# Layer 1: where the tap and slab transfers are issued, and how far TensorE's sums run behind the scan

## What is computed

```python
x = conv_general_dilated(x, conv_w, padding=((2, 2), (2, 2)), feature_group_count=C)
x = silu(x + conv_b[None, :, None, None])
xs = x.reshape(B, C, L)
x_dbl = einsum('kd,bdl->bkl', x_proj_w, xs)
dts, Bs, Cs = x_dbl[:, :R], x_dbl[:, R:R + N], x_dbl[:, R + N:]
delta = softplus(einsum('dr,brl->bdl', dt_w, dts) + dt_b[None, :, None])
log_dA = maximum(delta[:, :, None, :] * A[None, :, :, None], LOG_EPS)
P = exp(cumsum(log_dA, axis=-1))
dB_u = delta[:, :, None, :] * Bs[:, None, :, :] * xs[:, :, None, :]
hs = P * cumsum(dB_u / maximum(P, EPS), axis=-1)
y = einsum('bdnl,bnl->bdl', hs, Cs) + xs * Ds[None, :, None]
```

## Time and profile before

| what | us |
|---|---|
| median of 3 runs | 4020.88 (4011.57 to 4022.5) |
| the profiled execution, own time | 4020.36 |
| its span | 4018.6 |
| of it layer 0 and the start of layer 1 | about 1956 |
| scans of groups 0 to 6, each | 252.9 to 262.3 |
| scans of group 7, behind the loop | 246.9 |

### The profile page before, as it was taken

One profiled execution on the slowest core, in us unless ns is written; L12 is line 12 of the kernel. 1 busy time (PEld: TensorE's weight loads), 2 busy tenths in 40 slices (PEclk: granted clock), 3 DMA queues, 4 the chain that ended last, 5 costly groups with the idle time before them and its releaser, 6 DMA issues. The chain is left out here.

```text
span 4018.6 us, 72697 instructions
## 1 busy us (share of the span) xinstructions
PE 3650.8 (91%) x22358; PEld 2646.6 (66%) x22358; DVE 3106.0 (77%) x4416; ACT 2571.1 (64%) x4292; POOL 2575.8 (64%) x2672
## 2 busy tenths in 40 slices
PE   6999999999999999997899998998989989899776
PEld 6888787979787887877565564664646646466322
DVE  3675758475756667570499998999989989989999
ACT  1463728172735546274688787787778878777754
POOL 0352717162634536270488888888979889888988
PEclk9999999999999999998799898998989989989877
DMA  7546473747465554428565564655546646465222
GB/s 225 170 138 204 104 250 95 251 102 234 109 200 149 164 181 125 149 76 181 130 177 143 162 170 124 172 152 147 164 127 181 169 125 173 129 168 158 86 75 60
DMA packets 383746, 612.84 MB, mean 153 GB/s; under 512 B 199967, under 2 KB 324152, under 8 KB 383048
## 3 DMA queue, kind: packets, MB, share of 16 engines
q1 hardware_dynamic: 383336, 607.74, 53.5%
HBM read 527.35 MB, written 80.28 MB: 151 GB/s over the span
## 5 line engine op out<-in xcount | busy, mean ns | idle before, releaser
L321 POOL TENSOR_TENSOR h_low<-act_h,h_high 128x448 fp32r<-128x448 f32 x448 | 598.0, 1354 | 724.1 <-ACT h_high L520 723.9
L515 ACT ACTIVATE act_h<-ps_up,b 128x448 f32<-128x448 f32 x672 | 408.7, 635 | 728.5 <-PE ps_up L633 728.2
L1348 PE MATMUL ps_y<-h,ident 128*128 128x448 f32 x1344 | 727.1, 629 | 144.3 <-POOL h L1036 113.1
L1036 POOL TENSOR_TENSOR h<-h,c_rows 128x448 f32<-128x448 f32 x672 | 763.7, 1136 | 51.2 <-DVE h L1126 5.7
L1023 POOL TENSOR_TENSOR u<-dxs,b_rows 128x448 f32<-128x448 f32 x672 | 764.5, 1138 | 27.9 <-DVE ps_q L1115 16.8
L1099 DVE TENSOR_TENSOR_SCAN ps_q<-d_a,q_last,ps_q 128x448 f32<-128x448 f32 x576 | 659.5, 1145 | 0.0
L1126 DVE TENSOR_TENSOR_SCAN h<-d_a,h_last,ps_q 128x448 f32<-128x448 f32 x576 | 645.3, 1120 | 0.0
L1300 PEld LDWEIGHTS ps_front<-win,taps 120*112 120x112 f32 x4608 | 540.5, 188 | 149.2 <-issue 147.2
L606 PE MATMUL ps_stage<-win,taps 124*112 124x112 f32 x6144 | 608.3, 261 | 2.7 <-DVE w_low L368 2.7
L606 PEld LDWEIGHTS ps_stage<-win,taps 124*112 124x112 f32 x6144 | 608.1, 178 | 3.2 <-DVE w_low L368 2.8
L1205 ACT ACTIVATE d_a<-delta,log_eps,a_neg 128x448 f32<-128x448 f32 x672 | 503.3, 750 | 114.0 <-DVE h L1126 58.5
(11 more groups left out here) (81 smaller groups left out, 6212.6 us busy)
## 6 DMA issues: line engine op xcount, KB each, us to landing
taps<-in_t_dram SPq DMA_DIRECT2D x192, 896.0 KB, 5.0
taps<-in_t_dram SPq DMA_DIRECT2D x192, 672.0 KB, 4.7
b_rows<-bc_dram SPq DMA_DIRECT2D x224, 224.0 KB, 3.0
c_rows<-bc_dram SPq DMA_DIRECT2D x224, 224.0 KB, 3.1
xres<-in_x_dram SPq DMA_DIRECT2D x224, 168.0 KB, 2.5
x_dram<-x1o SPq DMA_DIRECT2D x224, 168.0 KB, 2.0
x1pad<-x_dram SPq DMA_DIRECT2D x96, 392.0 KB, 6.0
out_dram<-y SPq DMA_DIRECT2D x168, 224.0 KB, 2.6
```

Of the source, the lines that this page charges most:

```text
L321: nc.gpsimd.tensor_tensor(h_low[u % 2][:, t, :], act_h[u % 2][:, t, :], h_high[u % 2][:, t, :], ALU.subtract).then_inc(h_low_ready[t], 1)
L515: nc.scalar.activation(act_h[u % 2][:, t, :], ps_up[t][:, 0:BT], ACT.Gelu, bias=b1[:, t:t + 1]).then_inc(gelu_done, 1)
L1036: nc.gpsimd.tensor_tensor(h[s % H_SLOTS][:, :], h[s % H_SLOTS][:, :], c_rows[n][:, :], ALU.mult).then_inc(hc_done, 1)
L1348: nc.tensor.matmul(total, ident[:, :], h[s % H_SLOTS][:, :], start=False, stop=(n == N - 1)).then_inc(y_added, 1)
```

## The change

Three things change, in layer 1 alone. (1) A slab or tap load is no longer put into SyncE's list five steps ahead in any case, but at `begin_at`: five steps ahead, or the step after the slot's last user is scheduled to be done, whichever is later; the list is sorted by that. (2) In a step, these loads stand at the end, behind the row store, the row loads and the store of y. (3) Y_LAG is 3: TensorE sums, ScalarE's copies of y and the stores of y move one step later. The skip matmul keeps its step (s % 4 = 2), now in a function of its own, behind the sum of that step. The last two stores of a group stand at its end.

```diff
--- before.py
+++ after.py
@@ -80,7 +80,7 @@
 U_SLOTS = 3
 U_AHEAD = U_SLOTS
 H_SLOTS = 6
-Y_LAG = 2
+Y_LAG = 3
 Z_SLOTS = 2
 DA_SLOTS = 7
 DA_LEAD = 5
@@ -952,17 +952,21 @@
                 for load, k, _ in loads[:SLABS]:
                     load(f, False, k)
 
+            def begin_at(load, k, unit):
+
+                last_use = {load_slab: turn_unit, load_taps: conv_unit}[load]
+                slots, pieces = {load_slab: (SLABS, 1), load_taps: (SLOTS2, HALVES)}[load]
+                free = unit_step[last_use[k - slots]] + pieces + 1 if k >= slots else 0
+                return max(unit_step[unit] - AHEAD, free)
+
             def group(g, ahead, first=False):
 
-                todo = loads[SLABS:] if ahead else []
+                todo = sorted(loads[SLABS:], key=lambda load: begin_at(*load)) if ahead else []
                 for s in range(S):
                     b, j = s // STEPS, s % STEPS
                     f, fb = next_band(g, b)
                     if ahead == 2 and s == S - 2 * STEPS:
                         first_slabs(g + 2)
-                    while todo and unit_step[todo[0][2]] <= s + AHEAD:
-                        load, k, _ = todo.pop(0)
-                        load(g + 1, False, k)
                     if ahead or b + 1 < BANDS:
                         if j == STORE_XD_AT:
                             store_xd(f, fb)
@@ -974,7 +978,11 @@
                         load_c(g, b, LOAD_C_NOW[j])
                     if s >= N + Y_LAG + 1 and (s - N - Y_LAG - 1) % N == 0:
                         store(g, (s - N - Y_LAG - 1) // N)
-                store(g, RUNS - 1)
+                    while todo and begin_at(*todo[0]) <= s:
+                        load, k, _ = todo.pop(0)
+                        load(g + 1, False, k)
+                for r in range(RUNS - 2, RUNS):
+                    store(g, r)
 
             assert last > 1
             first_slabs(1)
@@ -1335,15 +1343,17 @@
                 nc.tensor.matmul(z[:, 0:BT], dtw[:, t, :], xd[:, :],
                                  start=True, stop=True).then_inc(z_done, 1)
 
+            def skip_y(g, r):
+
+                b, t = r // TILES, r % TILES
+                pe.wait_ge(y_kept, g * RUNS + max(r - Y_SLOTS + 1, 0) + 1)
+                nc.tensor.matmul(ps_y[r % Y_SLOTS][:, 0:BT], skip[:, t, :], xs[:, t, b * BT:(b + 1) * BT],
+                                 start=True, stop=False)
+
             def add_y(g, s):
 
-                b, t, n = s // STEPS, s % STEPS // N, s % N
-                r = b * TILES + t
-                total = ps_y[r % Y_SLOTS][:, 0:BT]
-                if n == 0:
-                    pe.wait_ge(y_kept, g * RUNS + max(r - Y_SLOTS + 1, 0) + 1)
-                    nc.tensor.matmul(total, skip[:, t, :], xs[:, t, b * BT:(b + 1) * BT],
-                                     start=True, stop=False)
+                n = s % N
+                total = ps_y[s // N % Y_SLOTS][:, 0:BT]
                 pe.wait_ge(hc_done, g * S + s + 1)
                 nc.tensor.matmul(total, ident[:, :], h[s % H_SLOTS][:, :],
                                  start=False, stop=(n == N - 1)).then_inc(y_added, 1)
@@ -1359,6 +1369,8 @@
                             front_waits(g + 1, i)
                     if s >= Y_LAG:
                         add_y(g, s - Y_LAG)
+                    if s % N == Y_LAG - 1:
+                        skip_y(g, s // N)
                     if burst:
                         for i in burst:
                             back(g if s == 0 else g + 1, i)
```

## The result

The changed kernel takes 4042.2 us, the median of 5 runs (4039.39 to 4052.35), beside 4022.5 us (4011.57 to 4038.22) for the kernel before, run in between. The ratio is 1.0056, with a 95% interval of 1.0032 to 1.0081: slower by about half a per cent, where 4015 us was forecast and the range ended at 4031. The ratios are not quotients of the two medians; each leaves out executions more than 1.5% above the quickest of their kernel, which drops four of twelve for the loads with the logarithm in front, one of twelve for the last kernel with an extra matmul, and none elsewhere. The profiled execution took 4039.4 us (span 4037.6), against 4020.4 us before.

The account below looks back on a forecast made before the run. VectorE's scans plus stops, ended by ScalarE's logarithm, were taken as the bound. Gains of 3.7 + 1.0 us at steps 8 to 20 and 1.0 at step 72, 5.7 off 4020.4, gave 4014.7, said as 4015; range 3995 to 4031.

Parts of the forecast that it names:

- The reading of what bounds the kernel: VectorE bounds each group, plus its stops; at step 7 the last wait to end is ScalarE's logarithm, not GpSimd's u.
- rival 1: VectorE's waits for u count in full: 36.1 us off, 3984 us; chance 0.12.
- The rows of C on time: GpSimd's wait for rows of C falls from 113.8 to under 20 us; VectorE gains 0, the logarithm covering it.
- Slabs and taps later: Slab and tap loads issued later, in the head and last third, still land in time: 0 us.
- The buffers of h: Behind the burst, near step 65, scans wait some 1 us for a buffer's sum; covered by later waits, so 0.
- Step 72: The burst's wait for a sum held by GpSimd goes; ScalarE's table load limits the gain to 0.14 us, times 7 = 1.0.
- Steps 36 to 71: set by the waits at 32 and 56, 0: TensorE's waits there are set by VectorE's delta through ScalarE's copy, so one sum fewer ahead gains 0.
- idles longer, and goes on at the same time: At steps 32 and 56 TensorE arrives 0.9 us sooner, waits 2.9 us in place of 2.0, and resumes unchanged.
- the gain of 3.7 + 1.0 us at steps 8 to 20: One sum fewer ahead of the turns saves 0.92 us in each of four slow heads, and 1.0 us in group 4.
- The forecast's own mark for being wrong from the ground up: ScalarE's chain from its first kept turn to the logarithm at step 7 taking other than 11.4 us.
- ScalarE is not waiting for TensorE: At step 7 in all seven groups ScalarE works without waiting for turns, so fewer sums gain 0.
- Rival 3: TensorE idles longer at steps 8, 32 and 56 and pays in clock; three more slow heads, 4031 us; chance 0.12.

Follow-up runs that it names:

- the last kernel with an extra matmul: Changed kernel with y copy and logarithm in front, plus one more matmul on TensorE in step 2 of every group: 4035.5 us, ratio 1.0003 (0.9968 to 1.0038).

## Why the prediction was wrong

**The reading of what bounds the kernel** held. The last wait to end is ScalarE's logarithm, and the loads alone gained 9 us by their ratio (17 at the end of its interval), not the 36.1 us of the u waits: rival 1 is out by the result and by the loads' own run.

**The rows of C on time** held: 16.9 us, under the 20 that I gave; the u waits went to 0 and took the logarithm's name. **Slabs and taps later** held too, no turn or convolution of groups 0 to 6 waits for a transfer. **The buffers of h**: one wait of 0.99 us at step 65, in group 2, followed by the one for the logarithm. **Step 72** held: ScalarE's table load ends at 2974.72 in group 3 and the first silu starts at 2974.73; in all seven groups the 0.14 us between them are down to 0.01.

**Step that failed first:** "Steps 36 to 71: set by the waits at 32 and 56, 0", and with it that TensorE "idles longer, and goes on at the same time". Its wait grew from 2.0 to 2.6 us, but not because it comes sooner: with the same three steps of lag and the copy in front the wait is 1.98 to 2.00 us in all seven groups, as before, and with two steps of lag and the copy late it is 2.60. In group 1 TensorE is through with the work ahead of the wait 2.17 us after the start of the decay that waited for delta in the kernel before, 2.03 us after it in the changed kernel, and 2.16 with the copy in front. So the sum fewer ahead gave next to nothing there, and the growth is the copy's: TensorE goes on 0.5 us later after delta. I had followed the sums on TensorE and the stores on SyncE to their new steps, and not the y copy on ScalarE, which the same number moves. Of a moved step every instruction counts; this one moved from ahead of a wait to behind it, on the very engine that I had named as the bound. Priced from rows of before it would have been a copy of about 0.6 us, twice a group. What it cost is 0.7 us a group at step 43 (9.9 against 5.2 us for seven groups) and, at steps 65 to 68, the difference between little and much time at half clock, 2.6 us by the kernel before's own groups 1 and 2. In the trace before, four of seven groups had paid that already, so the sum rose by 3.7 us only, from 22.9 to 26.6. The run with the copy in front has the short time in all seven and so takes off more than was lost: 18.9 us, from 9.9 + 26.6 to 6.5 + 11.1 us.

**Second:** the gain of 3.7 + 1.0 us at steps 8 to 20. Steps 9 to 23 lose 26.6 us where they lost 22.3. I took the number of slow heads as given and only priced what a sum less brings in each. They went from four to six, and the fall came 3 us sooner in the group, so that step 7, which I had called untouched, paid 34.2 us in place of 29.1. The forecast's own mark for being wrong from the ground up was a chain of other than 11.4 us (by its rows 2758.90 - 2747.44 = 11.5) from the first kept turn to step 7's logarithm. It is 2244.00 - 2231.48 = 12.5 us in group 1, and 11.5 us in group 5, the one head that kept its clock until 24.6 us. So "ScalarE is not waiting for TensorE" at step 7 failed as well: the order was as I had it, and the wait for the turn at half clock is the 1.01 us more.

**Rival 3** had the sign and six heads for its mark, and 4031 us. It was right in part. At step 56 the longer wait does go with more time at half clock, though the wait grew by the copy and not by TensorE's coming sooner. In the head it placed the mechanism wrongly. There TensorE had been busy for 13.10 of the 13.10 us ahead of the fall in group 1; the idle 5.69 us lay before that and were 5.42 us in the kernel before. The Trainium skill, "TensorE: Matmul & The Clock Gate", section "HAM oscillation", puts the half clock down to idle gaps between bursts. By that rule the fall in the head should not come, and this trace disagrees there; at steps 32 and 56 it agrees, with half clock behind waits of 2.57 to 2.60 us in the changed kernel. The same page, section "Part 1: The HAM clock gate", says that the gate runs free of the program, so that one kernel shows different counts of slow matmuls. With that the runs agree as far as they go: executions of one kernel spread over 62 us, the slower ones at a lower mean clock, and in one trace the fall comes at different times in groups that do the same work.

**What stays open.** Why the clock falls at 21 us in one order and at 24 in another, with TensorE without a gap in both. No run here tells it; the runs show only which turn pays for it. One rival is untested: of the 7.0 us ahead of the fall in group 1 TensorE spent 4.2 us on turns, which are small transposes, and a sum fewer changes the mix. No run replaced them by other work.

## What to carry to other kernels

- A lag between two engines moves everything that is placed by it. List its instructions on every engine, and ask of each whether it crosses a wait; here one 0.6 us copy behind a wait for delta, in place of ahead of it, cost 0.25% by itself (1.0025), while for the late rows of C, repaired alone, no gain is shown.
- An instruction whose input is ready is worth trying ahead of those that wait for a slower engine. Moving the logarithm ahead of the turns' copies was worth 1.2% on the changed kernel (1.0056 to 0.9932) and nothing on the kernel before (1.0004); moving its first half too, whose input is not ready, cost 2.4% (1.0164 against 0.9923).
- Where executions differ because TensorE's clock falls here or there, a trace of one execution gives the mechanism but not the mean. Compare traces by the stretch that was edited: here the untouched part ahead of it varied by 17.6 us. Count the slow heads as an outcome with its own chances, not as a fact of the kernel.
